# Cross-attention block on one core: Q kept in two orders, h written in order, products placed one by one, all orders written anew

## The reference

```python
h = layernorm(x, ln1_g, ln1_b)
x = attention(h, h, sa_wq, sa_wk, sa_wv, sa_wo, sa_bo) + x        # self attention
h = layernorm(x, ln2_g, ln2_b)
x = attention(h, cond_emb, ca_wq, ca_wk, ca_wv, ca_wo, ca_bo) + x # cross attention
h = layernorm(x, ln3_g, ln3_b)
p = h @ ff_w1 + ff_b1;  a, gate = p[..., :D_FF], p[..., D_FF:]
out = a * gelu(gate) @ ff_w2 + ff_b2 + x

def attention(xq, xkv, wq, wk, wv, wo, bo):
    q, k, v = xq @ wq, xkv @ wk, xkv @ wv          # cut into 16 heads of 64
    attn = softmax(einsum('bihd,bjhd->bhij', q, k) * 64 ** -0.5)
    return einsum('bhij,bjhd->bihd', attn, v).reshape(B, S, 1024) @ wo + bo
```

## Time and profile before

| | |
|---|---|
| median of 3 runs | 1268.66 us (1267.77 to 1270.17) |
| profiled execution | 1266.97 us, span 1264.9 us |
| PE busy | 1218.8 us, 96% of the span, 9385 matmul records |
| DVE, POOL, ACT busy | 777.8, 743.6, 625.5 us |
| TensorE clock granted | 0.999 over the span |
| costliest PE lines | 855 (P) 233.8 us self + 58.5 us cross; 839 (S) four groups of 102 to 109 us; 816 (X) 120.6 us |

### The profile page before, as it was taken

The page is one execution under the profiler, slowest core; times in us unless marked ns, Lnnn a source line. Parts: engine busy times, 40 slices in busy tenths (PEclk is TensorE's granted clock), DMA queues, the critical chain, the costliest instruction groups (busy, mean ns, idle before and its releaser), DMA issues.

```text
span 1264.9 us, 23491 instructions
## 1 busy us (share of the span) xinstructions
PE 1218.8 (96%) x9385; PEld 833.5 (66%) x9385; DVE 777.8 (61%) x1289; ACT 625.5 (49%) x890; POOL 743.6 (59%) x381
## 2 busy tenths in 40 slices
PE   5999999999999999999999999999999999989998
PEld 4666665666666666656666665666766666668887
DVE  5767556566566576665665665457677767664433
ACT  4457543444444455744444444446755475535432
POOL 2388686686785785966867868854555335320000
PEclk9999999999999999999999999999999999999999
DMA  3000000000000000000000100021111110000000
GB/s 111 23 1 14 22 2 14 10 14 14 2 22 14 1 23 13 2 22 14 2 22 2 27 6 5 22 67 27 32 40 27 48 30 15 11 22 18 18 18 17
DMA packets 63538, 25.75 MB, mean 20 GB/s; under 512 B 34551, under 2 KB 61383, under 8 KB 63431
## 3 DMA queue, kind: packets, MB, share of 16 engines
q1 hardware_dynamic: 63375, 24.25, 7.4%
q10 hardware_dynamic: 56, 0.01, 0.0%
HBM read 21.62 MB, written 2.10 MB: 19 GB/s over the span
## 4 chain that ended last, share of the span: by engine, by line
PE 82%; DVE 9%; ACT 5%; issue 3%; POOL 1%; DMA 1%; SPq 0%; DVEq 0%; POOLq 0%; ACTq 0%
PE psum L855 21%; PE psum L839 19%; PE psum L732 13%; PE psum L715 9%; PE psum L816 6%; PE psum L878 5%; DVE xr L1079 5%; PE psum L938 3%; PE psum L821 2%; PE psum L866 2%; DVE q_lo L1034 2%; ACT h_hi L1188 1%; ACT probs L1258 1%; ACT q_hi L1236 1%; POOL acc L1387 1%
## 5 line engine op out<-in xcount | busy, mean ns | idle before, releaser
L1387 POOL TENSOR_TENSOR acc<-acc,probs 128x1024 f32<-128x1024 f32 x192 | 458.5, 2388 | 81.1 <-ACT probs L1258 69.2
L1258 ACT ACTIVATE probs<-psum 128x1024 f32<-128x1024 f32 (+1 forms) x320 | 319.4, 1027 | 292.6 <-PE psum L839 292.6
L1042 DVE TENSOR_REDUCE m_part<-psum 128x2 f32<-128x1024 f32 x256 | 310.1, 1224 | 244.9 <-PE psum L816 244.7
L1387 POOL TENSOR_TENSOR acc<-probs 128x1024 f32<-128x1024 f32 (+1 forms) x64 | 153.3, 2395 | 183.2 <-PE psum L866 95.4
L855 PE MATMUL psum<-probs,val 128*64 128x512 f32 x1024 | 233.8, 598 | 0.0
L1079 DVE SCALAR_TENSOR_TENSOR xr<-psum,d_cols,xr 128x256 f32<-128x256 f32 x512 | 207.5, 477 | 34.9 <-PE psum L878 33.7
L855 PEld LDWEIGHTS psum<-probs,val 128*64 128x64 f32 x1024 | 67.8, 136 | 125.2 <-issue 123.3
L839 PE MATMUL psum<-row_max,minus 64*128 64x512 f32 (+1 forms) x640 | 128.4, 391 | 0.0
L816 PE MATMUL psum<-k_hi,q_hi 64*128 64x512 f32 x512 | 120.6, 480 | 3.2 <-DVE m_part L1042 1.0
L816 PEld LDWEIGHTS psum<-k_hi,q_hi 64*128 64x128 f32 x512 | 79.6, 306 | 63.6 <-issue 52.0
L839 PE MATMUL psum<-q_hi,k_hi 64*128 64x512 f32 x512 | 109.1, 417 | 6.8 <-DVE xr L1079 3.0
(11 more groups left out here) (144 smaller groups left out, 2107.3 us busy)
## 6 DMA issues: line engine op xcount, KB each, us to landing
xr<-in_x SPq DMA_DIRECT2D x8, 256.0 KB, 6.4
wv_raw<-in_L_xattn_sa_wv SPq DMA_DIRECT2D x8, 256.0 KB, 2.9
wqk_raw<-in_L_xattn_sa_wq SPq DMA_DIRECT2D x16, 128.0 KB, 2.4
wqk_raw<-in_L_xattn_sa_wk SPq DMA_DIRECT2D x16, 128.0 KB, 2.4
wo_raw<-in_L_xattn_sa_wo SPq DMA_DIRECT2D x16, 128.0 KB, 2.4
d_cols<-d_rows SPq DMA_DIRECT2D x128, 2.0 KB, 2.1
wqk_raw<-in_L_xattn_ca_wq SPq DMA_DIRECT2D x16, 128.0 KB, 2.6
probs<-in_L_xattn_ff_w SPq DMA_DIRECT2D x8, 256.0 KB, 3.5
```

Source lines behind the costliest of these rows:

```text
L1042: dve.tensor_reduce(m_part[:, half, :, t, kh], psum[:, bank0:bank0 + 2, :], AX.X, ALU.max).then_inc(s_x_read, 1)
L1258: act.activation(probs[buffer_of(J, u)][0:plan.ks, :, :], psum[0:plan.ks, bank0:bank0 + 2, :], ACT.Exp, scale=SCALE).then_inc(s_exp, 1)
L1387: pool.tensor_tensor(total, last if kt == 1 else total, now, ALU.add).then_inc(s_acc, 1)
```

## The change

- **Q a second time.** After `q_hi`, ACT copies the same PSUM once more, sorted by tile, into `turned(J)` (`qx` in self, a new tile `q_turned_late` in cross). It is one more 128x512 activation per half of Q, 64 in all. X takes its weights from there in one piece, and waits for `s_turned` instead of `s_hi`. DVE's `q_lo`, which frees Q's PSUM buffer, also waits for `s_turned`.
- **h in order.** `affine` and `h_low` (first four normalisations) write SBUF in one piece and read PSUM with a stride of 128 elements.
- **P by the unit.** `units_of` goes; each P on PE's list is one unit.
- **Memory.** The two cross value tiles move into the second half's place, so V16 waits until all P of J=15 are done.
- **Orders.** Every order text is new, apart from `SLOT`, `NORM_AT` and `FF_AT`.

```diff
+        q_turned_late = sb("cross_q_turned", [P, SEQ], F32R)
+        cval = [sb(f"cross_val{b}", [CROSS.ks, CROSS.kt, DM]) for b in range(2)]
+        def turned(J):
+            return qx[J % 2] if plan_of(J) is SELF else q_turned_late
+        def by_row(ap):
+            return ap.rearrange("k (p t) -> k p t", t=4)
+        def across(ap):
+            return ap.rearrange("k (t p) -> k p t", t=4)
@@ def X(J, a):                                   # TensorE
-                q, _ = queries(J)
+                q = turned(J)
-                    pe.wait_ge(s_hi, KQ0[J] + plan.khalf + 1 + a // 8)
+                    pe.wait_ge(s_turned, 2 * J + 1 + a // 8)
-                mm = pe.matmul(bank(bank0 + h), q[r, half * HALF + t:(half + 1) * HALF:4], k_hi[...])
+                mm = pe.matmul(bank(bank0 + h), q[r, half * HALF + t * P:half * HALF + (t + 1) * P], k_hi[...])
@@ def PV
-                for u in units_of(J, g):
+                half, kt = u // plan.kt, u % plan.kt
@@ def h_low / def affine
-                    lo, full, hi = tiled(lo), in_tiles(full), tiled(hi)
+                    lo, full, hi = by_row(lo), across(full), by_row(hi)
-                    h, rows = tiled(h), in_tiles(rows)
+                    h, rows = by_row(h), across(rows)
@@ def KQ                                          # VectorE
+                if kind == "Q":
+                    dve.wait_ge(s_turned, 2 * J + a + 1)
@@ def Q                                           # ScalarE
                 act.activation(queries(J)[0][:, cols], psum[:, prep, :], ACT.Copy).then_inc(s_hi, 1)
+                if plan_of(J) is SELF:
+                    act.activation(in_tiles(turned(J)[:, cols]), tiled(psum[:, prep, :]), ACT.Copy).then_inc(s_turned, 1)
+                else:
+                    every = turned(J)[:].rearrange("k (t p) -> k t p", t=8)[:, :, a * DH:(a + 1) * DH]
+                    act.activation(every, psum[:, prep, :].rearrange("k (p t) -> k t p", t=8), ACT.Copy).then_inc(s_turned, 1)
@@ def V                                           # ScalarE
-                    act.wait_ge(s_pv, U0[2 * (G - 1)])
+                    act.wait_ge(s_pv, U0[2 * (G - 1) if plan is SELF or J > NSELF else NSELF])
```

More of the change, by code:

```diff
@@ L62, in __init__ @@
         self.vkt = 2
-        self.group = 4
         self.probs = 12 if own else 4
@@ L179 @@
+    "pool": "b0@64.90 b1@124.07",
 }
 TURN = {
[L181 to L187 removed]
@@ L260 @@
 ORDER = {e: stream(e) for e in ("sp", "pe", "dve", "act", "pool")}
-def units_of(J, g):
-    group = plan_of(J).group
-    return range(g * group, (g + 1) * group)
 def item_of(kind, J, a):
@@ L815, in X @@
                         r = rows_of(h)
-                        mm = pe.matmul(bank(bank0 + h), q[r, half * HALF + t:(half + 1) * HALF:4], k_hi[r, kh * HALF:(kh + 1) * HALF], start=True, stop=True)
+                        mm = pe.matmul(bank(bank0 + h), q[r, half * HALF + t * P:half * HALF + (t + 1) * P], k_hi[r, kh * HALF:(kh + 1) * HALF], start=True, stop=True)
                 else:
@@ L840, in S, with PV @@
                 mm.then_inc(s_s, 1)
[L842 removed]
+            def PV(J, u):
                 plan = plan_of(J)
[L844 to L857 removed]
+                half, kt = u // plan.kt, u % plan.kt
+                pe.wait_ge(s_exp, U0[J] + u + 1)
+                if kt == 0:
+                    after(pe, s_o_lo, 2 * (J - 1) + half + 1)
+                    if half == 0 and J % 2 == 0:
+                        wait_release(pe, ("V", J + 1 if plan is SELF else J, 0))
+                for h in range(2):
+                    d = slice(h * DH, (h + 1) * DH)
+                    own = slice(J % 2 * P + h * DH, J % 2 * P + (h + 1) * DH)
+                    mm = pe.matmul(psum[d, PVB + half, :], values(J)[0:plan.ks, kt, own], probs[buffer_of(J, u)][0:plan.ks, h, :],
+                                   start=(kt == 0), stop=(kt == plan.kt - 1))
+                mm.then_inc(s_pv, 1)
             def D(J):
```

98 lines of the change are left out of this document (44 added, 54 removed), and 59 rows, old and new, of tables (OPENING, SELF_ORDER).

## The result

The changed kernel takes **1225.38 us** (median of 4 runs, 1225.27 to 1225.93); the kernel before takes 1268.68 us on the same chip. The ratio is 0.9664 (95% interval 0.9653 to 0.9676): 43.3 us faster. The forecast was 1248.5 us, about 20 us faster, with a range that ended at 1226: the change did twice what I said and lies just outside my range. The profiled span went from 1264.9 to 1223.4 us.

The account below looks back on a forecast made before the run. PE's own list was taken as the bound: work, changes of tile, buffer waits. Self -19, cross -4.5 and opening +3.3 took 1266.97 to 1247 us; with 1.7 us offset the forecast was 1248.5 us, range 1226 to 1268.

Parts of the forecast that it names:

- X contiguous, self: Self attention: contiguous weights save 0.11 us at four X behind P or D, about 0.1 at one more: -0.55 us per iteration.
- X contiguous, cross: Cross attention: weight loads set X's time, so contiguous weights save 0.9 us per iteration, bounds 0.5 and 1.1; -14 us in all.
- Changes of tile: Stretches of P or D go from 81 to 150, 0.35 us each: +1.05 us per self iteration, +6.6 us in cross.
- Waits, self: PE's waits for PSUM buffers in a self iteration: 1.7 of 2.4 us go, bounds 0 and 2.4.
- Normalisations: Time of the normalisations, taken together with the turn: change 0, bounds -4 and +4 us.
- Turn: The turn from self to cross attention, taken together with the normalisations: change 0, bounds -4 and +4 us.
- Waits, cross: Cross iterations without V: K and S2 wait for buffers, 0.4 us in each of eight: +3 us, bounds 0 and +8.
- Longer life of Q's buffer: Q's buffer returns 1.2 us later: just covered in self, if not up to 0.5 us per iteration; covered in cross.
- Feed-forward is untouched: The feed-forward part after the iterations was said to stay as it was, change 0.
- h in order: ACT's writes of h fall from 1117 ns to 0.8 us; off PE except four opening writes, -0.3 us each.
- Opening: Start up to K0: the context first on PE's list starts t0.0 4.7 us later; net +3.3 us, bounds 0 and +5.
- Rival 3: All waits go and X gains where nothing was given: self -30, cross -10, opening +1 us; 1229 us, chance 0.17.

## Why the prediction was wrong, point by point

- **X contiguous, self** (-0.55 us per iteration): right in its price. 0.45 became 0.33, loads 306 became 188 ns, and nothing was gained where the load was covered. In the new orders, with seven X behind P or D, it is worth 1.0 us an iteration.
- **X contiguous, cross** (-0.9): 0.71 measured.
- **Changes of tile** (0.35 us each): right, 0.36 measured.
- **Waits, self** (-1.7): this term of the sum was mis-sized. The plain self iteration changed by -1.75 us, where -0.55 + 1.05 leave 2.25 of the 2.4 us for the waits: practically all went. I had walked the list, found 0.3 us left and then took 0.7 "for what a walk misses". The walk had missed nothing. Over eleven plain iterations this is 6.1 of the 23 us by which I was off. That the waits went because of the places of P is shown by the runs with P in fours and with one P merged.
- **Normalisations** (0, with the turn bounds -4 and +4): the step that failed most. J=1 and 9 changed by 3.6 us more than the share that I gave them, and J=18, 19, 26 and 27 by 6.3: 9.9 us. In cross attention it was the new places: 3.9 us of idle in front of the transposes were in the trace of before, and I read none of them. In self attention it was h in order, which I had called "off PE, except in the opening": 1.0 us in each of J=1 and J=9, where an X waited for `h_lo` (0.50 and 0.47 us of idle in the trace of before, 1.02 and 0.99 with the orders alone, 0.14 now).
- **Turn** (in the same 0): near it. J=15 lost 4.1 us, but J=16 and 17 gained 1.6, together 2.5 less, where I gave them 1.8. Why work moved from one to the other is read from the traces only.
- **Waits, cross** (+3 us) and changes of tile there (+6.6): measured together they are near nothing. The new orders with the old code have 17.74 us against 17.67 before, +0.07 where the two terms make +0.6. Which of the two was too large is not told apart. With X's 0.71 instead of 0.9 this leaves 3.0 us over eight plain iterations.
- **Longer life of Q's buffer**: covered, and with more to spare than the 0.3 us that I saw. But it is real: 1.2 us per iteration under the old orders.
- **"Feed-forward is untouched"** (0): false. One Y moved behind F1, and 4.8 us went. A list "before/after" of only one middle iteration hid the move from me.
- **h in order**: 0.8 taken, 0.78 measured. The rule on PSUM lines that I weighed (the Trainium skill, "SBUF — State Buffer", which says it of matmuls), carried over to copies, would have made a stride of 128 slow; it is not so: ScalarE's other write with scale and bias, contiguous in PSUM, takes 751 ns (line 1196). That h would matter in J=1 and 9 too I had not seen.
- **Opening** (+3.3): +7.0. The context and the write of h came nearly as forecast; what I missed was the moved memsets and subtraction of GpSimd beside z1 (3.0 us, shown) and the clock, at half from 35.0 to 41.8 us; every run with this opening has such a stretch.

Another 1.7 us of the 23 are the offset that I added between the profiled execution and the median: the changed kernel has none (1225.46 and 1225.38).

Rival 3 ("all waits go, and X gains where I gave nothing", 1229 us, chance 0.17) is nearest: all waits of the plain self iteration went. X gained nothing more, though, and that its sum fits is in part luck. Its terms were self -30 us (measured -31.9), cross -10 (-11.8), opening +1 (+7.0) and nothing for the tail (-4.7); in the first two the normalisations make up what it had too much elsewhere, and the last two nearly cancel.

## What to carry to other kernels

When an engine's list is the bound, add up the waits at each place that the new order touches, the rare iterations and the tail included: here the plain iterations of both kinds gave 24.5 of the 41.5 us. A short piece of work placed in front of an item that would wait is worth its change of tile: here 0.35 us hid 0.95 to 1.2 us, and some longer waits were followed by the clock at half as well. And a layout change that lengthens a buffer's life should be timed together with the order that covers it, since alone it showed nothing (0.9994), part of which was the clock behind the waits that it made.
